# A layered kernel whose last attention stage adds its causal mask on DVE instead of by products on PE

## The chip, the cores and the metric

The kernel runs on one core of one Trainium2 chip. The metric is the device time of one execution in microseconds (us). PE is the matrix engine, DVE the vector engine, ACT the activation engine, POOL the GpSimd engine and SP the engine that issues most DMAs. PSUM, the memory that PE writes its products to, is used as eight banks, each of 512 float32 per partition.

## The reference, cut to what matters

Four layers follow each other on x of 4 batches x 1024 positions x 128 channels: x = x + attention(norm(x)) + feed-forward(norm(x)). The change is in the last layer, whose attention has 16 heads of 8 channels and a causal mask, beside a mixture of 8 experts with the two best per token:

```python
# layer 3: b = 4, s = 1024, h = 16, hd = 8
qkv = (x @ W_qkv + b_qkv).reshape(b, s, h, 3 * hd)
...
logits = jnp.einsum('bshd,bkhd->bhsk', q, k) / np.sqrt(hd)
mask = k_pos > q_pos
logits = jnp.where(mask[None, None, :, :], -jnp.inf, logits)
attn = jax.nn.softmax(logits, axis=-1)
out = jnp.einsum('bhsk,bkhd->bshd', attn, v).reshape(b, s, d)
return out @ W_out + b_out
```

## The kernel before, in words

`layer3` runs a norm, a front stage that makes q, k, v and the routing of the experts, and `attn3_stage`, where attention, experts and output projection run together. All of the change is in `attn3_stage`.

The attention is cut into 16 items: 4 batches, each with 4 groups of 4 heads. An item passes through three slots, so that slot s has three items in work. In slot s the *first pass* of item s makes the scores of each query against the keys that it may see, and takes the largest of each row. In slot s + 1 the maxima are turned (`turn_max`, `turned_max`), split into three bfloat16 parts on POOL (`split_max`) and sent by DMA into extra rows of the q tile. In slot s + 2 the *second pass* makes the same scores the other way round, keys on the partitions and the maximum already subtracted by those extra rows (`scoreT`, L2194); ACT takes the exponential (`exps`, L2329), POOL zeroes what is masked on the diagonal (`causal`, L2509), and PE sums with v (`sums`, L2209). So there are 18 slots: slots 0 and 1 have only a first pass (and in slot 1 the turn of the maxima), slots 2 to 15 have both passes, slots 16 and 17 only the second.

The first pass of an item is 20 units (S0 to S19 below). A unit is one tile of 128 queries (t = 0 to 7) against up to 512 keys, for two row groups r of the array (partitions 0 to 63 and 64 to 127, `HROW`), and for one or both of two head pairs e. PE (`score`, L2167) writes a unit into two neighbouring banks; DVE (`largest`, L2379) reduces it with one maximum. Units S0 and S1 (t = 0, 1), S8 (the last 128 keys of t = 4) and S11 (the last 256 of t = 5) hold both e; S2 to S5, S14, S15, S18 and S19 are diagonal units of one e. These 12 of 20 units end on the diagonal: their last 128 keys hold a square in which the keys above the diagonal are in the future. In it, before the change, PE adds the mask with four more products per e (L2172): identity times `maskneg_q` (-1e30 above the diagonal, else 0), in two halves of 64 rows, for each r. The constants for it are loaded by four DMAs and cast to bfloat16 by POOL.

The order on each engine is written out by hand. A slot has 12 groups g; `SHARE` says how many units of the first pass stand in each: 2, 2, 1, 1, 2, 2, 2, 2, 2, 2, 1, 1. Between them stand the second pass, and, in slots 2 to 13, the 39 expert tiles: `turn_rows` (XT, at the start of the slot, read by the DVE copy L2406), `up` (a burst after group 4, L2236, followed by `gelu` on ACT with an activation table of its own), and `down` (groups 7 to 10, L2246, read by the DVE copy L2412). `turn_sums` (X, L2218) turns an item's result for `norm` on DVE (L2394, L2399).

Two rings of banks tie the engines. The S ring has two places of two banks each, and everything that DVE reads goes through it in one order: Z (the turned maxima), the S units, XT, X, DOWN and the output projection. Before PE writes entry n of this ring it waits until DVE has read entry n - 2. The other ring has three banks, between PE's second pass and ACT. Every engine runs its instructions in order, so a PE instruction that waits for DVE also holds back the second-pass products behind it. The next slot begins with Z, which waits for the reduction over the maxima (`a_m`, L2470), and this for the last unit.

Of the kernel before, what the change touches and what calls it, by code (L numbers as in the profile page):

```python
# [18 lines left out]
BF16 = mybir.dt.bfloat16  # L19
# [3 lines left out]
P = 128  # L23
# [75 lines left out]
class Kit:  # L99
# [14 lines left out]
    def sb(self, name, shape, dt=F32, ctx=None):  # L114
        return (ctx or self.ctx).enter_context(self.nc.sbuf_tensor(name, shape, dt))
# [1798 lines left out]
HROW = (0, 64)  # L1914
# [86 lines left out]
def attn3_stage(k, R):  # L2001
# [15 lines left out]
    with ExitStack() as ctx:  # L2017
        sb = lambda x, shape, dt=F32: k.sb("a3_" + x, shape, dt, ctx=ctx)
        qs = [sb(f"q{u}", [P, 2, S], BF16) for u in range(4)]
        ks = [sb(f"k{u}", [P, 2, S], BF16) for u in range(4)]  # L2020
        consts, constsb = sb("consts", [P, 2, 2, P]), sb("consts_bf16", [P, 2, 2, P], BF16)
        mx = sb("mx", [P, 2, 2, 2, QT, 2])
        m = sb("m", [P, 2, 2 * 2 * QT])
        mT, mr = sb("mT", [32, 2, P]), sb("mr", [32, 2, P])
# [38 lines left out]
        with nc.Block() as block:  # L2063
            @block.sync
            def _(sp):
                for r in range(2):
                    for n, src in enumerate(("ident", "maskneg_q")):
                        sp.dma_start(consts[HROW[r]:HROW[r] + 64, n, :, :],
                                     ins[src].rearrange("(a p) q -> p a q", p=64)).then_inc(s_c, 16)
                for dst, src in ((wo[:], ins["L3a_wout"]), (b2[0:NE], ins["L3f_b2"]),  # L2070
                                 (b2[NE:NE + 1], ins["L3a_bout"].rearrange("(a n) -> a n", a=1))):
                    sp.dma_start(dst, src).then_inc(s_o, 16)
# [51 lines left out]
                for s in range(SLOTS):  # L2124
# [8 lines left out]
                        store_tile(kt)  # L2133
                    if 3 <= s + 2 < NI:
                        stacks(s + 2)
                sp.wait_ge(s_c, 64)
                sp.wait_ge(s_o, 48)
                for u in range(4):
                    sp.wait_ge(s_qk[u], 16 * 4 * len(RUNS) * NI // 4)
# [3 lines left out]

            @block.tensor
            def _(pe):
                pe.wait_ge(ready, 9)
                pe.wait_ge(o_zero, 1)

                def take_s(*key):
# [6 lines left out]
                def score(c, i):  # L2156

                    t, es, x, w = SU[i]
                    u = c % 4
                    if i == 0:  # L2160
                        pe.wait_ge(s_qk[u], 16 * 4 * len(RUNS) * (c // 4 + 1))
                    bank = take_s("S", c, i)
                    diag = x + w == (t + 1) * P
                    for j, e in enumerate(es):
                        for r in range(2):
                            rows = slice(HROW[r], HROW[r] + KROWS)
                            mm = pe.matmul(k.ps[:, bank + r, j * w:j * w + w], qs[u][rows, e, t * P:t * P + P],  # L2167
                                           ks[u][rows, e, x:x + w], start=True, stop=not diag, skip_group_check=True)
                        for half in range(2 if diag else 0):
                            for r in range(2):  # L2170
                                rows = slice(HROW[r], HROW[r] + 64)
                                mm = pe.matmul(k.ps[:, bank + r, j * w + w - P:j * w + w],  # L2172
                                               constsb[rows, 0, half, :], constsb[rows, 1, half, :],
                                               start=False, stop=half == 1, skip_group_check=True)
                    mm.then_inc(s_done, 1)

                def turn_max(c):
# [181 lines left out]
            def _(dve):  # L2359
                dve.memset(k.ps[:, bankO, :], 0.0).then_inc(o_zero, 1)  # L2360
                dve.memset(mx[:], -3e38).then_inc(mx_zero, 1)
                dve.wait_ge(mx_zero, 1)
                n_i = itertools.count(1)
                last = {}

                def arrived(*key):

# [4 lines left out]
                def largest(c, i):  # L2372

                    t, es, x, w = SU[i]
                    if i == 0 and c >= 2:
                        dve.wait_ge(max_done, c - 1)
                    bank = arrived("S", c, i)
                    src = k.ps[:, bank:bank + 2, 0:len(es) * w].rearrange("p r (e k) -> p r e k", k=w)
                    dve.tensor_reduce(mx[:, c % 2, :, es[0]:es[0] + len(es), t, x // CH], src, AX_X, ALU.max)\  # L2379
                       .then_inc(s_read, 1)  # L2380

# [94 lines left out]
            def _(pool):  # L2476
                for u in range(4):
                    for r in range(2):
                        pool.memset(ks[u][HROW[r] + 32:HROW[r] + 64, :, :], 1.0).then_inc(ready, 1)
                        pool.wait_ge(ready, 2 * u + r + 1)  # L2480
                pool.wait_ge(s_c, 64)
                pool.tensor_copy(constsb[:], consts[:]).then_inc(ready, 1)
                n_p = itertools.count(1)

                def split_max(c):

                    def step(one):
                        one.then_inc(split, 1)
                        pool.wait_ge(split, next(n_p))

                    u = c % 2
                    if c == 0:
                        pool.wait_ge(ready, 9)
                    if c >= 2:
                        pool.wait_ge(masked, (c - 1) * len(DIAG))
                    pool.wait_ge(s_read, s_at["Z", c] + 1)
                    if c > 0:
                        pool.wait_ge(s_m[(c - 1) % 4], 16 * 6 * ((c - 1) // 4 + 1))
                    step(pool.tensor_copy(mp[:, 0, :], mT[:, u, :]))
                    step(pool.tensor_tensor(mr[:, 0, :], mT[:, u, :], mp[:, 0, :], ALU.subtract))  # L2500
                    step(pool.tensor_copy(mp[:, 1, :], mr[:, 0, :]))
                    step(pool.tensor_tensor(mr[:, 1, :], mr[:, 0, :], mp[:, 1, :], ALU.subtract))
                    pool.tensor_copy(mp[:, 2, :], mr[:, 1, :]).then_inc(parts, 1)
# [185 lines left out]
```

## Time and profile before

| | us |
|---|---|
| median of 3 runs | 2866.93 |
| lowest and highest | 2866.49 to 2872.39 |
| the profiled execution's own time | 2862.31 |
| its span, first to last instruction | 2860.6 |
| attention stage: first unit to the end of slot 15's first pass | 2061.0 to 2750.1 |

Mean granted TensorE clock 0.846 of full speed. The span lies 1.7 us under the execution's own time, and that execution lies 4.6 us under the median. A row of the timeline gives start, duration, engine, line, operation, the tiles (out<-in) with shapes and how many instructions are merged; a bracket says how long the engine was idle just before and which instruction ended it. A row of a stretch gives the busy time of each engine in it, and the granted clock.

### The profile page before, as it was taken

To read this page: it belongs to the slowest core of one execution; us is meant where nothing else is said; L and a number is where in the kernel's file an instruction comes from. 1 tells how busy PE (TensorE), PEld (TensorE's weight loads), DVE (VectorE), ACT (ScalarE), POOL (GpSimd) and SP (SyncE) were. 2 spreads that over 40 slices of the span, in tenths; PEclk is the share of its full clock that TensorE was granted. 3 is DMA by queue.
4 is the path that set the end of the run, shared out by engine and by line. 5 is a ranking of instruction groups with operands and counts; after the bars stand their busy time and mean duration, and the time that the engine had idled before them with its cause. 6 is when DMAs were issued, how large, how long until landed. Compare 5 with 4: busy or idle time off the path is not lost. (4 is left out here: it accounts for less than half of the span.)

```text
span 2860.6 us, 35232 instructions
## 1 busy us (share of the span) xinstructions
PE 2053.1 (72%) x10366; PEld 1065.6 (37%) x10366; DVE 1900.9 (66%) x2468; ACT 1428.5 (50%) x2507; POOL 1366.1 (48%) x990
## 2 busy tenths in 40 slices
PE   2698787897977668566635888851178888888875
PEld 1233333333333244243414666641034444444312
DVE  6299999999999966833256777762175555555641
ACT  1476677777767527133414333323036556656453
POOL 2299989998999940220024666517201111111353
PEclk9899999998999979687766888965569999999866
DMA  1344444444545520012100000004222222222111
GB/s 31 88 152 143 154 148 139 155 153 137 157 140 156 152 63 0 1 52 72 37 0 0 0 0 0 0 11 99 82 61 80 75 72 81 66 79 57 35 26 49
DMA packets 146983, 214.72 MB, mean 75 GB/s; under 512 B 30746, under 2 KB 58292, under 8 KB 146228
## 3 DMA queue, kind: packets, MB, share of 16 engines
q1 hardware_dynamic: 142756, 204.72, 23.7%
q0 software_dynamic: 4096, 8.40, 1.4%
q8 instruction: 64, 1.05, 0.2%
q14 instruction: 67, 0.55, 0.1%
HBM read 193.91 MB, written 23.86 MB: 76 GB/s over the span
## 5 line engine op out<-in xcount | busy, mean ns | idle before, releaser
L513 PE MATMUL ps<-m_hC,ident 128*128 128x512 f32 x1024 | 510.2, 642 | 136.6 <-DVE m_hC L795 136.6
L711 POOL TENSOR_TENSOR m_dBx<-m_du,m_rowB 128x1024 f32<-128x1024 f32 x256 | 603.8, 2387 | 7.0 <-DMA m_rowB<-bc_rows 6.8
L2329 ACT ACTIVATE a_pT<-ps 128x512 f32<-128x512 f32 (+2 forms) x640 | 319.7, 553 | 398.1 <-PE ps L2194 396.7
L2379 DVE TENSOR_REDUCE a_mx<-ps 128x2 f32<-128x1024 f32 (+2 forms) x320 | 349.3, 1116 | 168.8 <-PE ps L2172 128.1
L637 ACT ACTIVATE ps<-m_delta,m_A 128x512 f32<-128x512 f32 x512 | 339.7, 685 | 120.2 <-DVE m_h L786 119.3
L513 PEld LDWEIGHTS ps<-m_hC,ident 128*128 128x128 f32 x1024 | 202.2, 205 | 429.4 <-issue 229.0
L2509 POOL TENSOR_SCALAR_AFFINE_SELECT a_pT<-a_pT 128x512 f32<-128x512 f32 x128 | 81.5, 636 | 522.8 <-ACT a_pT L2329 522.3
L786 DVE TENSOR_TENSOR_SCAN m_h<-ps,m_carry,m_dBx 128x512 f32<-128x512 f32 x256 | 311.2, 1266 | 9.0 <-ACT ps L637 9.0
L786 DVE TENSOR_TENSOR_SCAN m_h<-ps,m_dBx 128x512 f32<-128x512 f32 x256 | 295.9, 1206 | 18.8 <-ACT ps L637 18.2
L795 DVE TENSOR_TENSOR m_hC<-m_h,ps 128x1024 f32<-128x1024 f32 x176 | 214.9, 1221 | 23.0 <-ACT ps L647 7.2
L721 POOL TENSOR_TENSOR m_hC<-m_h,m_rowC 128x1024 f32<-128x1024 f32 x80 | 194.4, 2430 | 71.0 <-DVE m_h L786 70.7
L2167 PE MATMUL ps<-a_k,a_q 48*128 48x512 bf16 (+3 forms) x768 | 141.0, 369 | 110.7 <-DMA a_k<-qk_parts 94.3
L2209 PE MATMUL ps<-a_pT,l_v 128*9 128x512 f32 (+3 forms) x1536 | 189.6, 570 | 22.6 <-POOL a_pT L2509 22.6
L2194 PE MATMUL ps<-a_q,a_k 51*128 51x512 bf16 (+3 forms) x768 | 131.4, 367 | 68.7 <-ACT a_pT L2329 67.3
L647 ACT COPY ps<-m_rowC 128x512 f32<-128x512 f32 x176 | 102.9, 585 | 126.6 <-DVE m_hC L795 125.9
L1629 PE MATMUL ps<-c_triu_adt,ones 128*128 128x512 f32 x64 | 53.6, 934 | 92.0 <-ACT c_triu_adt L1600 92.0
L468 PE MATMUL ps<-pad,m_wk 128*128 128x512 f32 x256 | 117.3, 603 | 1.1 <-DVE m_diag L744 1.1
L2194 PEld LDWEIGHTS ps<-a_q,a_k 51*128 51x128 bf16 x768 | 32.6, 95 | 193.8 <-ACT a_pT L2329 158.3
L266 PE MATMUL ps<-ident,n_xn 128*128 128x128 f32 x128 | 35.3, 431 | 84.2 <-DVE n_xn L246 83.8
L1907 POOL DMA_INDIRECT expert_rows<-l_xn,l_slot x64 | 65.3, 1020 | 62.0 <-DVE p_cmp L1873 42.8
L1078 POOL TENSOR_TENSOR acc<-acc,b_o 128x512 f32 x8 | 11.2, 1402 | 170.8 <-ACT acc L1068 170.8
L2167 PEld LDWEIGHTS ps<-a_k,a_q 48*128 48x128 bf16 x768 | 40.2, 100 | 130.4 <-issue 94.8
(361 smaller groups left out, 3927.8 us busy)
## 6 DMA issues: line engine op xcount, KB each, us to landing
m_rowB<-bc_rows SPq DMA_DIRECT2D x256, 256.0 KB, 4.5
m_rowC<-bc_rows SPq DMA_DIRECT2D x256, 256.0 KB, 4.0
a_w<-in_L3f_w1T SPq DMA_DIRECT2D x39, 256.0 KB, 2.5
a_w<-in_L3f_w2T SPq DMA_DIRECT2D x39, 256.0 KB, 3.2
qk_parts<-p_part SPq DMA_DIRECT2D x24, 256.0 KB
expert_rows<-in_zero_rows SPq DMA_DIRECT2D x39, 128.0 KB, 2.7
a_xs<-expert_rows SPq DMA_DIRECT2D x39, 128.0 KB, 2.1
expert_out<-a_y SPq DMA_DIRECT2D x39, 128.0 KB, 3.2
```

The lines of the kernel that those rows point to most:

```text
L468: mm = pe.matmul(o, wk[:, d, tap, c * P:c * P + P], pad[:, b * ROW + shift:b * ROW + shift + CH], start=tap == 0, stop=tap == CONV - 1)
L513: mm = pe.matmul(ps[:, bankY + c, :], k.ident[:], hC[:, n % NBUF, c, :], start=False, stop=n % NS == NS - 1)
L637: act.activation(ps[:, bankA + m % 3, :], delta[:, i % 2, c, chunk(i, x)], ACT.Exp, scale=An[:, ITEMS[i][0], c, s:s + 1]).then_inc(decayed, 1)
L711: pool.tensor_tensor(dBx[:, n % NBUF], du[:, i % 2, :, chunk(i, x)], rowB[:, n % 4, :].unsqueeze(1).to_broadcast([P, HALF, CH]), ALU.mult) ...
L721: pool.tensor_tensor(hC[:, n % NBUF], h[:, n % NBUF], rowC[:, n % 4, :].unsqueeze(1).to_broadcast([P, HALF, CH]), ALU.mult).then_inc(hc_po ...
L786: dve.tensor_tensor_scan(time(h[:, n % NBUF, c, :]), time(ps[:, bankA + m % 3, :]), time(dBx[:, n % NBUF, c, :]), first, ALU.mult, ALU.add ...
L795: dve.tensor_tensor(hC[:, n % NBUF], h[:, n % NBUF], ps[:, bankC, :].unsqueeze(1).to_broadcast([P, HALF, CH]), ALU.mult).then_inc(hc_dve, 1)
L2167: mm = pe.matmul(k.ps[:, bank + r, j * w:j * w + w], qs[u][rows, e, t * P:t * P + P], ks[u][rows, e, x:x + w], start=True, stop=not diag, ...
L2194: mm = pe.matmul(k.ps[:, tbank(n + r), j * w:j * w + w], ks[u][rows, e, kt * P:kt * P + P], qs[u][rows, e, q0:q0 + w], start=True, stop=Tr ...
L2209: mm = pe.matmul(k.ps[32 * hd:32 * hd + HD + 1, bankO, CH - w:CH], R["v"][:, c, kt, hd, :], pT[:, g % 3, hd, 0:w], start=kt == 0, stop=kt ...
L2329: act.activation(dst, src, ACT.Exp).then_inc(t_read, 1)
L2379: dve.tensor_reduce(mx[:, c % 2, :, es[0]:es[0] + len(es), t, x // CH], src, AX_X, ALU.max)\
```

## The change

PE's mask products, their constants, the four DMAs and POOL's cast are gone. The mask is loaded once in float32. DVE, before the maximum of each of the 12 diagonal units, adds the mask to the square in the score banks (PSUM in, PSUM out) with one instruction for both r and the e of the unit, waits for its own result, and then reduces as before. 192 additions in 16 items take the place of 1024 products in the records.

```diff
-        consts, constsb = sb("consts", [P, 2, 2, P]), sb("consts_bf16", [P, 2, 2, P], BF16)
+        maskneg, hidden = sb("maskneg", [P, P]), k.sem("a3_hidden")
...
-                for r in range(2):
-                    for n, src in enumerate(("ident", "maskneg_q")):
-                        sp.dma_start(consts[HROW[r]:HROW[r] + 64, n, :, :],
-                                     ins[src].rearrange("(a p) q -> p a q", p=64)).then_inc(s_c, 16)
+                sp.dma_start(maskneg[:], ins["maskneg_q"]).then_inc(s_c, 16)
...
-                pe.wait_ge(ready, 9)
+                pe.wait_ge(ready, 8)
...
-                                           ks[u][rows, e, x:x + w], start=True, stop=not diag, skip_group_check=True)
-                        for half in range(2 if diag else 0):
-                            for r in range(2):
-                                rows = slice(HROW[r], HROW[r] + 64)
-                                mm = pe.matmul(k.ps[:, bank + r, j * w + w - P:j * w + w],
-                                               constsb[rows, 0, half, :], constsb[rows, 1, half, :],
-                                               start=False, stop=half == 1, skip_group_check=True)
+                                           ks[u][rows, e, x:x + w], start=True, stop=True, skip_group_check=True)
...
+                dve.wait_ge(s_c, 16)
...
+                    if x + w == (t + 1) * P:
+                        square = src[:, :, :, w - P:w]
+                        future = maskneg[:].unsqueeze(1).unsqueeze(1).to_broadcast([P, 2, len(es), P])
+                        dve.tensor_tensor(square, square, future, ALU.add).then_inc(hidden, 1)
+                        dve.wait_ge(hidden, next(n_h))
...
-                pool.wait_ge(s_c, 64)
-                pool.tensor_copy(constsb[:], consts[:]).then_inc(ready, 1)
...
-                    if c == 0:
-                        pool.wait_ge(ready, 9)
```

On DVE, at the start of slot 3 (a slot with both passes and expert tiles), the order before is, with `a_mT` the turned maxima, `a_mx` the row maxima and `a_xT` the turned expert rows:

```order
L2386 TENSOR_SCALAR a_mT<-ps 32x128
L2379 TENSOR_REDUCE a_mx<-ps 128x4 x2
L2406 COPY a_xT<-ps 128x256
L2379 TENSOR_REDUCE a_mx<-ps 128x2 x2
L2406 COPY a_xT<-ps 128x256
L2379 TENSOR_REDUCE a_mx<-ps 128x2
L2406 COPY a_xT<-ps 128x256
```

and with the change (the same lines stand four to ten lines earlier in the file):

```order
L2382 TENSOR_SCALAR a_mT<-ps 32x128
L2373 TENSOR_TENSOR ps<-ps,a_maskneg 128x2x256
L2375 TENSOR_REDUCE a_mx<-ps 128x4
L2373 TENSOR_TENSOR ps<-ps,a_maskneg 128x4x128
L2375 TENSOR_REDUCE a_mx<-ps 128x4
L2402 COPY a_xT<-ps 128x256
L2373 TENSOR_TENSOR ps<-ps,a_maskneg 128x2x128
L2375 TENSOR_REDUCE a_mx<-ps 128x2
L2373 TENSOR_TENSOR ps<-ps,a_maskneg 128x2x128
L2375 TENSOR_REDUCE a_mx<-ps 128x2
L2402 COPY a_xT<-ps 128x256
```

Each of the diagonal units has an addition in front of its reduction; nothing else changes place. On PE, at the start of slot 2, the order before is, with L2180 the turn of the maxima and L2194 the second pass:

```order
L2180 MATMUL ps<-ident,a_m 32x128
L2194 MATMUL ps<-a_q,a_k 128x512 x2
L2167 MATMUL ps<-a_k,a_q 128x128 x2
L2172 MATMUL ps<-a_consts_bf 128x128 x4
L2167 MATMUL ps<-a_k,a_q 128x128 x2
L2172 MATMUL ps<-a_consts_bf 128x128 x4
L2194 MATMUL ps<-a_q,a_k 128x512 x2
```

and with the change:

```order
L2170 MATMUL ps<-ident,a_m 32x128
L2184 MATMUL ps<-a_q,a_k 128x512 x2
L2163 MATMUL ps<-a_k,a_q 128x128 x4
L2184 MATMUL ps<-a_q,a_k 128x512 x2
L2163 MATMUL ps<-a_k,a_q 128x256 x4
```

The mask products are gone, and the products around them follow each other directly.

## Rows read from the trace of the kernel before

**Rows 1.** The page, part 1: busy time, share of the span, instructions of each engine.

```profile
PE 2053.1 (72%) x10366; PEld 1065.6 (37%) x10366; DVE 1900.9 (66%) x2468; ACT 1428.5 (50%) x2507; POOL 1366.1 (48%) x990
```

**Rows 2.** Busy time of each engine by stretch, slots 0, 7, 14, 15. Columns: stretch, length, busy (instructions), clock, DMA.

```profile
2061.00:2083.40 22.40, 14.54 (x112) 5.66 (x112) 21.20 (x21) 0.00 (x0) 0.00 (x0) 0.50 0.18 56
2343.00:2385.60 42.60, 35.83 (x343) 18.47 (x343) 25.78 (x33) 27.99 (x56) 6.75 (x13) 1.00 0.22 62
2667.70:2712.10 44.40, 37.63 (x313) 15.52 (x313) 27.16 (x33) 20.92 (x42) 19.77 (x27) 0.85 0.14 39
2712.10:2750.10 38.00, 29.81 (x257) 8.81 (x257) 23.71 (x28) 20.84 (x42) 19.72 (x27) 0.78 0.10 26
```

**Rows 3.** All products of line L2172: duration ns min/median/max, first and last start.

```profile
L2172 PE MATMUL ps<-a_consts_bf x1024: 213/216/312, 2061.1 to 2748.4; 64*128 64x128 bf16 x171
```

**Rows 4.** DVE in slots 0 and 1, in order of time.

```profile
2062.74 20.49 DVE L2379 TENSOR_REDUCE a_mx<-ps 128x4 f32<-128x1024 f32 x19
...
2085.65 20.49 DVE L2379 TENSOR_REDUCE a_mx<-ps 128x4 f32<-128x1024 f32 x19 [0.16 <-PE ps L2172]
```

**Rows 5.** DVE timeline: what additions, waits and a write to PSUM take.

```profile
2035.15 0.48 DVE L2360 MEMSET ps<- 128x512 f32 x1 [35.49 <-PEq L1746]
...
2330.26 0.69 DVE L2426 TENSOR_TENSOR x_tm<-x_tm,ps 128x512 f32<-128x512 f32 x1 [2.90 <-PE ps L2270]
2330.87 2.35 DVE L2379 TENSOR_REDUCE a_mx<-ps 128x2 f32<-128x1024 f32 x2
...
2368.58 0.26 DVE L2394 RECIPROCAL a_rs<-ps 128x16 f32<-128x16 f32 x1 [0.33 <-PE ps L2218]
2368.88 0.29 DVE L2399 TENSOR_TENSOR a_att<-ps,a_rs 128x128 f32<-128x128 f32 x1
```

**Rows 6.** Start of slot 7, PE and DVE, in order of time.

```profile
2343.17 0.27 PE L2180 MATMUL ps<-ident,a_m 128*32 128x128 f32 x1 [0.82 <-DVE a_m L2470]
...
2343.48 0.28 DVE L2386 TENSOR_SCALAR a_mT<-ps 32x128 f32<-32x128 f32 x1 [0.45 <-PE ps L2180]
...
2344.22 0.69 DVE L2379 TENSOR_REDUCE a_mx<-ps 128x4 f32<-128x512 f32 x1 [0.46 <-PE ps L2172]
...
2345.33 1.23 DVE L2379 TENSOR_REDUCE a_mx<-ps 128x4 f32<-128x1024 f32 x1 [0.42 <-PE ps L2172]
...
2347.11 1.82 DVE L2379 TENSOR_REDUCE a_mx<-ps 128x2 f32<-128x768 f32 x2 [0.22 <-PE ps L2172]
...
2349.55 1.23 DVE L2379 TENSOR_REDUCE a_mx<-ps 128x2 f32<-128x1024 f32 x1 [0.24 <-PE ps L2172]
...
2350.83 0.66 PE L2218 MATMUL ps<-ident,a_oT 128*128 128x128 f32 x4 [0.20 <-DVE a_mx L2379]
...
2354.47 2.86 PE L2236 MATMUL ps<-a_xT,a_w 128*128 128x256 f32 x12
```

**Rows 7.** End of slot 7, PE and DVE.

```profile
2382.27 0.38 PE L2167 MATMUL ps<-a_k,a_q 48*128 48x512 bf16 x2
2382.49 0.28 PE L2172 MATMUL ps<-a_consts_bf 64*128 64x128 bf16 x4
...
2382.81 2.54 DVE L2379 TENSOR_REDUCE a_mx<-ps 128x2 f32<-128x1024 f32 x2 [0.24 <-PE ps L2172]
...
2385.75 0.27 PE L2180 MATMUL ps<-ident,a_m 128*32 128x128 f32 x1 [0.82 <-DVE a_m L2470]
```

**Rows 8.** Starts of slots 2, 7 (to the burst) and 14, stretches as in rows 2.

```profile
2106.50:2120.50 14.00, 13.18 (x111) 4.94 (x111) 8.78 (x12) 7.15 (x15) 4.21 (x9) 0.63 0.09 27
2343.10:2354.40 11.30, 9.87 (x123) 4.25 (x123) 9.13 (x14) 7.49 (x16) 4.21 (x9) 1.00 0.23 66
2668.00:2681.00 13.00, 8.92 (x117) 3.60 (x116) 9.21 (x11) 8.20 (x17) 10.27 (x16) 0.96 0.32 91
```

**Rows 9.** PE in slot 14, the same products at either level of the clock.

```profile
2681.14 1.11 PE L2255 MATMUL ps<-ident,a_att 128*128 128x128 f32 x4
...
2686.97 0.66 PE L2255 MATMUL ps<-ident,a_att 128*128 128x128 f32 x4
```

More of the change, by code:

```diff
@@ L2135, in _ @@
                         stacks(s + 2)
-                sp.wait_ge(s_c, 64)
+                sp.wait_ge(s_c, 16)
                 sp.wait_ge(s_o, 48)
@@ L2162, in score @@
                     bank = take_s("S", c, i)
-                    diag = x + w == (t + 1) * P
                     for j, e in enumerate(es):
@@ L2362, in _ @@
                 dve.wait_ge(mx_zero, 1)
-                n_i = itertools.count(1)
+                n_i, n_h = itertools.count(1), itertools.count(1)
                 last = {}
+                dve.wait_ge(s_c, 16)
                 def arrived(*key):
```

## The prediction

> **What bounds the kernel now.** I read the page's busy times first [rows 1]: over the whole span PE and DVE lead with 72% and 66%, so no average decides. The change touches only the last attention stage, so I cut that into its slots [rows 2]. Three kinds stand out. In slots 0 and 1 (first pass alone) DVE is busy 21.2 of 22.4 us, and its timeline shows 19 reductions without a gap in 20.49 us in each of the two [rows 4]: DVE is the bound, and PE waits for it. In slots 2 to 13, of which slot 7 is the type, PE is busy 35.8 of 42.6 us, DVE 25.8, ACT 28.0: PE's order is the spine, and it stops where ACT or DVE is late. Slots 14 and 15 have no expert tiles, but POOL, with 19.7 us, stands in PE's way. Then I read the start and the end of slot 7 in order of time [rows 6, 7]. At the start DVE has hardly any slack: between the turned maxima, read at 2343.76 (2343.48 + 0.28), and the reduction of unit S4 at 2350.78 (2349.55 + 1.23), it idles 0.46 + 0.42 + 0.22 + 0.24 = 1.34 us of 7.0, and PE's X (L2218) already waits 0.20 for it. Between the groups 5 and 10 it has much slack. At the end Z waits 0.82 us for the maxima.
>
> **What an addition costs.** No row shows an addition from PSUM into PSUM. The nearest one adds 512 elements from PSUM into SBUF in 0.69 us, a product of 128 elements takes 0.29 [rows 5]. The line through the first two gives 0.29 + 0.40 x 128/384 = 0.42 for 256. A diagonal unit of one e has 256 elements in its squares (2 r x 128), one of two e 512. The wait for its own result has a row too: the product of L2399 waits for the reciprocal in front, and starts 0.30 after the latter's start of 0.26, that is 0.04 after its end; two reductions without a wait start 2.35 - 1.23 = 1.12 apart, so 0.1 before the end of the first. The addition itself may start overlapped in that way; the reduction behind it may not. In a chain without gaps an addition therefore puts its duration and 0.04 on top: 0.46 for 256 elements and 0.73 for 512. An item has 8 of the first and 4 of the second: 3.7 + 2.9 = 6.6 us.
>
> The page "VectorE: DVE Perf Modes" of the Trainium skill (The DRAIN you can't avoid) says that the next operation waits for the pipe to empty anyway and that a semaphore in between costs nothing extra. The rows speak against it: 0.1 us of overlap without a wait, a gap of 0.04 with one. By the page an addition would put some 0.13 less on the chain, 1.6 us less an item, and the sum below would be about 10 us smaller; I go by the rows.
>
> The bounds of an addition: not under a write of 512 elements into PSUM alone, 0.48, and for 256 not under the 0.29 of the 128-element one [rows 5]; with the gap, 0.52 and 0.33, which is 4.7 us an item. Not over one that passes its elements twice, for reading and writing the same banks: 0.69 for 256 and 1.23 for 512 (the 1024-element reduction), with the gap 0.73 and 1.27, 10.9 us an item. I take 6.6, the same operation with another destination.
>
> **What PE gives back.** 1024 products of 216 ns [rows 3] overlap each other. What they add is how much later the last of them ends: in unit S18, 2382.49 + 0.28 = 2382.77 against 2382.27 + 0.38 = 2382.65 without [rows 7], 0.12 us per e. An item has 16 such e, 1.8 us at full clock.
>
> **Slots 0 and 1.** DVE's chain grows by 6.6 us in each, and all of it is on the path, since PE waits for the banks. At the start of either the mask products leave the front of the first reduction; with the clock at half (0.50, rows 2) they take about twice 0.12 per e, so 0.4 for the first unit and a little for the second. I count 6.2 + 6.0 = +12.2 us.
>
> **Slots 2 to 13, the start.** S0 to S4 bring two additions of 0.73 and three of 0.46: 2.8 us before S4 is read. Of the 1.34 us of idle time in this chain all close but 0.2 (DVE starts S0 that much after the turned maxima are read): 1.1 us. So S4 is read 1.7 us later. PE's X is entry n + 2 of the ring and now waits for it; what stands behind X on PE, in order, is the second pass of groups 3 and 4, units S5 to S7 and the burst of expert products that starts at 2354.47 [rows 6]. ACT takes its scores from that second pass and gets them 1.7 late as well. The mask products taken off PE here buy nothing, as PE waits at each entry. +1.7.
>
> **The middle.** In groups 5 to 9 DVE waits for PE by microseconds, so the additions of S8, S11, S14 and S15 lie beside PE's work, but for 0.2 us at S12, which stands two entries behind S11. PE saves the masks of these units; at S8 and S14 a wait for ACT follows at once and takes the saving, at S11 and S15 (0.24 + 0.12) it stays: PE comes to S18 0.3 earlier (S12's 0.2 is caught within PE's wait for ACT behind it).
>
> **The end.** S18 and S19 bring 0.92 us of additions. 0.12 goes since S18 reaches DVE earlier, 0.2 since its two reductions have a gap between them (2.54 against 2.35 for two in a row, rows 7 and 5). So the maxima, and Z behind them, come 0.6 later; with the 0.3 saved upstream +0.3. A slot costs 1.7 + 0.3 = 2.0 us, twelve 24 us.
>
> **Slots 14 to 17.** POOL's mask and DMA issues hold PE up more than DVE does, and there is no XT. The additions hide, and PE at a lower clock (0.85 and 0.78, rows 2) keeps something of its 1.8 us: -1.5 in all. The rest is untouched. The removed cast and DMAs lie before the q and k stacks land, which is what PE's first product waits for: nothing. The mask's DMA lands long before the first unit.
>
> The sum of work is 12.2 + 24 - 1.5 = +34.7 us.
>
> **The clock.** It moves between 1.2 and 2.4 GHz. Slot 2 runs to its burst at a granted 0.63, mostly the lower level, and takes 14.0 us for what slot 7 does in 11.3 at 1.00 [rows 8]: 2.7 us. In slot 14 PE is busy 8.9 of the first 13 us, and right behind them the same four transposes take 1.11 instead of 0.66 us, the lower level [rows 8, 9]; 6 us later they are fast again. In slot 7 it is busy 9.9 us up to the burst; with the change the masks of S0 to S5 leave this stretch (8 e, 1.0 us) and it becomes 1.7 longer: 8.9 of 13 us, as in slot 14. So the clock may fall in slots 2 to 13 too, where it now stays up. What falls into the DVE-bound start costs nothing, what reaches the burst up to 2.7 us; ACT, with 4 to 5 us of gelu in it, covers part. I take 0.5 us a slot, +6, between 0 and 12 x 2.7 = 32.
>
> The forecast is +41 us: 2862.3 + 41 = 2903 for an execution like the profiled one, and, as that lies 4.6 under the median, 2908 for the median.
>
> **Rivals.**
> *The clock falls in every slot.* For it speaks slot 14, against it that slots 2 to 13 hold more PE work than slot 14 and that the fall may land where DVE is the bound. 34.7 + 32 = +67: 2934. The page "TensorE: Matmul & The Clock Gate" of the Trainium skill (Part 1) says that the throttled state is the default and that activity releases it; slot 14 agrees. It is this rival's rule.
> *PSUM to PSUM costs double.* 10.9 an item: slots 0 and 1 +8.6 more; S0 to S4 2 x 1.27 + 3 x 0.73 = 4.7 instead of 2.8, the end 0.5 more, 12 x 2.4 = 29. 41 + 38 = +79: 2946. For it speaks only that no row shows the form.
> *Faster: PE is the bound and DVE's slack swallows the additions.* DVE is idle 16.8 us in slot 7, more than 6.6. If the delay at a slot's start were caught up before Z, PE would keep 1.8 us in each of 14 slots, -25, against 12.2 in slots 0 and 1: -13, 2854. It decides the other way once S4's read is more than 0.2 us or so late, since X already waits for it; and for catching up the middle would need PE idle that is not ACT's.
> *No change.* Slots 2 to 15 give back just the 12.2 of slots 0 and 1: 0.9 us each, half of the masks; 2867.
>
> Chances: forecast 0.58, clock 0.20, double price 0.10, faster 0.05, no change 0.04, and 0.03 for more than +79. About 0.2% (5.7 us) is what a measurement of this kernel tells from no change. Slower 0.91, within 0.04, faster 0.05. Downwards the lower price takes 3.8 us off slots 0 and 1, and 0.8 at a start and 0.3 at an end, x 12 = 13, off the others, and a clock that stays up takes off 6: 2885 for both together. The forecast's own range is 2890 to 2930. To hold 8 in 10 it takes in the clock rival: 2890 to 2938.
>
> **What would show it.** Right: L2373 takes 0.42 and 0.69 us; slots 0 and 1 are 6 us longer each; in slots 2 to 13 X (now L2208) waits 1 to 2 us for DVE, the burst starts 13 us after Z, and the slots are 2 to 3 us longer; slots 14 and 15 keep their length. Wrong: an addition of 1.2 us for 512 elements; granted clock under 0.9 in slots that had 1.00, with slots 4 us longer; or Z in slots 3 to 13 at its old distance, with DVE idle before it.

## The result, and the profile after

The changed kernel takes 2914.28 us (median of 4 runs, 2906.21 to 2920.22), the one before beside it 2868.38 (2866.49 to 2872.39). The ratio is 1.0156, 95% interval 1.0129 to 1.0184: slower by 46 us. The forecast was 2908 and 2890 to 2930. The profiled execution took 2915.11 with a span of 2913.4 us, so against the profiled one before the span is 52.8 us longer, where 41 were forecast. (Between executions of one kernel the clock of PE falls at different places.)

The page's busy times, to set beside [rows 1]:

```profile
PE 2062.0 (71%) x9342; PEld 1027.7 (35%) x9342; DVE 1994.7 (68%) x2660; ACT 1429.9 (49%) x2507; POOL 1365.8 (47%) x989
```

DVE gained 94 us of work and PE lost 1024 instructions, yet PE's busy time rose by 9: a product that runs at the lower clock counts for longer (0.61 us instead of 0.39 below). What an addition takes stands in the view of line L2373 (duration in ns, min/median/max), the operation that no row showed before:

```profile
L2373 DVE TENSOR_TENSOR ps<-ps,a_maskneg x192: 420/432/700, 2060.4 to 2800.1; 128x256 f32<-128x256 f32 x128, 128x512 f32<-128x512 f32 x64
```

0.42 to 0.43 us for 256 elements and 0.70 for 512, PSUM to PSUM, as the line through [rows 5] gave it. The slots, with the columns of [rows 2], again slots 0, 7, 14 and 15:

```profile
2061.00:2087.98 26.98, 10.31 (x40) 1.93 (x40) 26.45 (x33) 0.00 (x0) 0.00 (x0) 0.50 0.11 37
2369.78:2415.20 45.42, 36.83 (x279) 16.59 (x279) 31.63 (x44) 28.12 (x56) 6.75 (x13) 0.92 0.21 63
2717.38:2763.73 46.35, 38.76 (x249) 14.10 (x249) 32.92 (x44) 21.08 (x42) 19.91 (x27) 0.77 0.13 35
2763.73:2802.13 38.40, 29.11 (x201) 6.25 (x201) 29.58 (x39) 20.95 (x42) 19.99 (x28) 0.72 0.10 27
```

In slots 0 and 1 DVE has hardly a gap, and now an addition stands before each diagonal reduction:

```profile
2063.60 0.42 DVE L2373 TENSOR_TENSOR ps<-ps,a_maskneg 128x256 f32<-128x256 f32 x1
2064.05 0.96 DVE L2375 TENSOR_REDUCE a_mx<-ps 128x2 f32<-128x768 f32 x1
2064.93 0.42 DVE L2373 TENSOR_TENSOR ps<-ps,a_maskneg 128x256 f32<-128x256 f32 x1
...
2087.68 0.22 DVE L2466 TENSOR_REDUCE a_m<-a_mx 128x32 f32<-128x64 f32 x1
...
2116.07 0.22 DVE L2466 TENSOR_REDUCE a_m<-a_mx 128x32 f32<-128x64 f32 x1
```

From one addition to the reduction behind it pass 0.45 us, and the next addition starts 0.08 before that reduction ends: what [rows 4, 5] led to expect. The maxima of item 1 come 28.4 us after those of item 0, before 22.9.

The span's 52.8 us split as follows. Places are read from the two timelines: the first DVE instruction of the stage, the Z of each slot (L2180 before, L2170 after), the end.

| part | before | after | difference | forecast |
|---|---|---|---|---|
| all before the first unit is read | 2061.95 | 2060.39 | -1.6 | -0.4 |
| slot 0, first read unit to Z | 21.7 | 27.7 | +6.0 | +6.6 |
| slot 1 | 22.9 | 28.4 | +5.5 | +6.0 |
| slots 2 to 13 | 561.3 | 601.0 | +39.7 | +24 and 6 for the clock |
| slots 14 and 15 | 82.9 | 85.2 | +2.3 | -1.5 |
| behind them | 109.9 | 110.8 | +0.9 | 0 |

The first row is not the change: over the traces of all kernels in this document the first unit is read at 2052 to 2064 us, and in a second trace of the changed kernel (e9) at 2063.3.

The start of slot 7, PE first; the rows answer to [rows 6]:

```profile
2369.84 0.27 PE L2170 MATMUL ps<-ident,a_m 128*32 128x128 f32 x1 [1.50 <-DVE a_m L2466]
2370.04 0.39 PE L2184 MATMUL ps<-a_q,a_k 51*128 51x512 bf16 x2
...
2371.12 0.61 PE L2184 MATMUL ps<-a_q,a_k 51*128 51x512 bf16 x2 [0.57 <-ACT a_pT L2319]
...
2374.21 0.50 PE L2163 MATMUL ps<-a_k,a_q 48*128 48x384 bf16 x2 [0.46 <-DVE a_mx L2375]
...
2377.93 0.38 PE L2163 MATMUL ps<-a_k,a_q 48*128 48x512 bf16 x2
...
2380.11 0.65 PE L2208 MATMUL ps<-ident,a_oT 128*128 128x128 f32 x4 [0.66 <-DVE a_mx L2375]
...
2383.69 1.56 PE L2226 MATMUL ps<-a_xT,a_w 128*128 128x256 f32 x6
```

and DVE's additions in it:

```profile
2370.66 0.70 DVE L2373 TENSOR_TENSOR ps<-ps,a_maskneg 128x512 f32<-128x512 f32 x1 [0.23 <-PE ps L2163]
2371.39 0.69 DVE L2375 TENSOR_REDUCE a_mx<-ps 128x4 f32<-128x512 f32 x1
2372.20 0.70 DVE L2373 TENSOR_TENSOR ps<-ps,a_maskneg 128x512 f32<-128x512 f32 x1
...
2374.76 0.43 DVE L2373 TENSOR_TENSOR ps<-ps,a_maskneg 128x256 f32<-128x256 f32 x1 [0.27 <-PE ps L2163]
...
2378.36 0.43 DVE L2373 TENSOR_TENSOR ps<-ps,a_maskneg 128x256 f32<-128x256 f32 x1
2378.82 1.23 DVE L2375 TENSOR_REDUCE a_mx<-ps 128x2 f32<-128x1024 f32 x1
```

X (L2208) comes 10.3 us after Z instead of 7.7 and waits 0.66 for DVE; the burst (L2226) comes 13.9 after Z instead of 11.3. Z itself had waited 1.50 us for the maxima instead of 0.82. But a second thing is to be seen. The same pair of products of the second pass takes 0.39 us at 2370.04 and 0.61 at 2371.12, behind a wait of 0.57 for ACT: the clock has gone to its lower level, 1.3 us into the slot. At 2377.9 the products are fast again (0.38 for 512 columns). The stretch of 9.5 us from Z on shows it in its granted clock, here for slots 7 and 9, with all of slot 9 behind them:

```profile
2369.84:2379.34 9.50, 8.47 (x57) 2.40 (x57) 7.98 (x13) 5.51 (x11) 3.00 (x8) 0.64 0.24 72
2462.94:2472.44 9.50, 8.57 (x51) 2.32 (x55) 7.25 (x12) 5.07 (x11) 2.94 (x7) 0.50 0.40 112
2462.94:2516.78 53.84, 46.30 (x305) 21.16 (x306) 32.91 (x46) 29.80 (x60) 6.75 (x13) 0.81 0.23 66
```

and, for comparison, the start of slot 7 and the whole of slot 9 in the kernel before:

```profile
2343.17:2352.67 9.50, 8.61 (x109) 3.98 (x111) 7.40 (x12) 6.03 (x13) 3.78 (x9) 1.00 0.28 79
2429.60:2476.21 46.61, 39.96 (x370) 22.10 (x370) 26.61 (x34) 29.64 (x60) 6.75 (x13) 1.00 0.28 77
```

Before, 9 of the 11 starts of slots 3 to 13 had a granted clock of 1.00; after, none had (0.50 to 0.67). The end of slot 7, to set beside [rows 7]:

```profile
2411.58 0.43 DVE L2373 TENSOR_TENSOR ps<-ps,a_maskneg 128x256 f32<-128x256 f32 x1
...
2412.05 1.23 DVE L2375 TENSOR_REDUCE a_mx<-ps 128x2 f32<-128x1024 f32 x1
...
2413.19 0.42 DVE L2373 TENSOR_TENSOR ps<-ps,a_maskneg 128x256 f32<-128x256 f32 x1
...
2413.64 1.23 DVE L2375 TENSOR_REDUCE a_mx<-ps 128x2 f32<-128x1024 f32 x1
...
2415.27 0.37 PE L2170 MATMUL ps<-ident,a_m 128*32 128x128 f32 x1 [1.45 <-DVE a_m L2466]
```

The two reductions now have an addition before each, and Z comes where the addition of S19 puts it.

### The profile page after: what moved, and what is told of

Read it like the earlier page. It is cut to its first block and busy times, and to the rows that moved or that the text cites. A ratio compares the mean times of both kernels' runs of the same rounds, so it can differ in the third digit from the quotient of the medians.

```text
span 2913.4 us, 33371 instructions
## 1 busy us (share of the span) xinstructions
PE 2062.0 (71%) x9342; PEld 1027.7 (35%) x9342; DVE 1994.7 (68%) x2660; ACT 1429.9 (49%) x2507; POOL 1365.8 (47%) x989
## 3 DMA queue, kind: packets, MB, share of 16 engines
q1 hardware_dynamic: 142324, 204.53, 23.3%
## 5 line engine op out<-in xcount | busy, mean ns | idle before, releaser
L2375 DVE TENSOR_REDUCE a_mx<-ps 128x2 f32<-128x1024 f32 (+2 forms) x320 | 351.7, 1117 | 39.6 <-PE ps L2163 31.6
L2199 PE MATMUL ps<-a_pT,l_v 128*9 128x512 f32 (+3 forms) x1536 | 208.7, 623 | 17.9 <-POOL a_pT L2501 16.4
L2184 PE MATMUL ps<-a_q,a_k 51*128 51x512 bf16 (+3 forms) x768 | 141.1, 394 | 77.3 <-ACT a_pT L2319 71.6
L2373 DVE TENSOR_TENSOR ps<-ps,a_maskneg 128x256 f32<-128x256 f32 (+1 forms) x192 | 99.1, 516 | 106.6 <-PE ps L2163 102.7
```

What stands on the lines that cost most here:

```text
L2184: mm = pe.matmul(k.ps[:, tbank(n + r), j * w:j * w + w], ks[u][rows, e, kt * P:kt * P + P], qs[u][rows, e, q0:q0 + w], start=True, stop=Tr ...
L2199: mm = pe.matmul(k.ps[32 * hd:32 * hd + HD + 1, bankO, CH - w:CH], R["v"][:, c, kt, hd, :], pT[:, g % 3, hd, 0:w], start=kt == 0, stop=kt ...
```

## The experiments

All variants of the mask keep both ways in one source and choose by unit: where PE masks, the products are those of before; where DVE masks, the addition of the change. "X" and "burst" below are times after Z in the profiled execution; "starts at 1.00" counts, in the 11 slots from 3 to 13, those whose first 9.5 us have a granted clock of 1.00. The sums were made by adding the slots of each trace. A ratio is taken beside runs of the kernel before on the same chip: e1 to e4 on one chip, e5 to e8 on a second, e9 to e12 on a third. The ratio is of all runs, the other columns are of one execution, which need not be a typical one: that of e2 took 2855.3 us where the median of its kernel is 2870.3, and that of e10 2894.0 where the median is 2903.8.

| kernel | ratio to before, 95% | starts at 1.00 | Z to burst, slots 2 to 13 | burst to next Z | slot 1 |
|---|---|---|---|---|---|
| before | 1 | 9 of 11 | 144.5 | 416.8 | 22.9 |
| changed | 1.0156, 1.0129 to 1.0184 | 0 | 170.4 | 430.6 | 28.4 |
| changed, again (e9) | 1.0150, 1.0120 to 1.0180 | 0 | 169.9 | 426.2 | 28.4 |
| both (e1) | 1.0166, 1.0136 to 1.0196 | 3 | 173.5 | 425.1 | 28.9 |
| neither (e2) | 1.0011, 0.9993 to 1.0028 | 2 | 152.2 | 412.6 | 22.0 |
| PE for items 0, 1 (e3) | 1.0148, 1.0113 to 1.0182 | 0 | 171.0 | 430.2 | 22.9 |
| DVE in the middle (e4) | 0.9999, 0.9981 to 1.0018 | 8 | 144.1 | 409.2 | 22.9 |
| changed, filled at Z (e5) | 1.0111, 1.0070 to 1.0153 | 0 | 169.0 | 416.5 | 28.7 |
| DVE at the start (e6) | 1.0059, 1.0033 to 1.0086 | 0 | 168.5 | 409.5 | 25.4 |
| DVE at the end (e7) | 1.0041, 1.0011 to 1.0071 | 2 | 158.4 | 423.6 | 23.8 |
| before, filled (e8) | 0.9962, 0.9937 to 0.9987 | 11 | 138.7 | 413.3 | 23.3 |
| changed, filled throughout (e10) | 1.0127, 1.0100 to 1.0153 | 8 | 169.3 | 414.9 | 28.7 |
| middle, filled (e11) | 0.9967, 0.9949 to 0.9984 | 11 | 139.4 | 410.7 | 23.3 |
| neither, filled (e12) | 0.9978, 0.9955 to 1.0001 | 4 | 148.7 | 412.9 | 22.4 |

### Both sides' work, and neither's

The theory after the result was that PE's waits for DVE bring the clock down (A); its rival, that the products PE lost do (B). Two kernels cross the factors: in one both functions below return True, in the other both False.

```diff
-                    diag = x + w == (t + 1) * P
+                    diag = x + w == (t + 1) * P and pe_masks(c, i)
...
+                    if x + w == (t + 1) * P and dve_masks(c, i):
+                        square = src[:, :, :, w - P:w]
...
+                        dve.tensor_tensor(square, square, future, ALU.add).then_inc(hidden, 1)
```

> PE keeps its mask products and DVE adds the mask as well (the mask is added twice, which leaves the same keys hidden). In the changed kernel the granted clock falls to its lower level at the start of nearly every slot from 2 to 13, and X there comes 10.2 to 11.0 us after Z instead of 7.7. Theory A: the fall comes from PE's waits for DVE (the longer wait of Z, the waits in the ring). Then it stays when PE has its products back: X at 10 to 11 us in most slots, time 2910 to 2930, ratio to before 1.015 to 1.022. Rival B: the fall comes from the products that PE lost. Then the clock stays up at the starts, X comes at 9.4 us (7.7 + 1.7 by DVE's work alone), and the time is 2895 to 2905, ratio 1.009 to 1.013.

> No mask at all in the first pass: no products on PE and no additions on DVE; the maxima are then taken over the future keys of the diagonal squares too, the second pass is untouched. Theory A: with nothing added to DVE, PE's waits are as before, the clock stays up at the starts, X comes at 7.4 to 7.7 us, a slot from 2 to 13 is 0.3 us shorter, and slots 0 and 1 are unchanged within 1 us: ratio 0.996 to 0.999. Rival B: PE's missing products let the clock fall at the starts as in the changed kernel, each costing about 2.6 us: ratio 1.005 to 1.010.

Both: 1.0166, inside A's range. But 3 of 11 starts kept their clock, and they show what both engines' work costs without a fall. Slot 4's first 9.5 us, and PE's waits in it:

```profile
2215.17:2224.67 9.50, 7.08 (x85) 3.00 (x85) 8.07 (x13) 5.47 (x11) 3.58 (x8) 1.00 0.35 102
```

```profile
2219.56 0.34 PE L2177 MATMUL ps<-a_k,a_q 48*128 48x384 bf16 x2 [1.16 <-DVE a_mx L2395]
...
2225.16 0.66 PE L2228 MATMUL ps<-ident,a_oT 128*128 128x128 f32 x4 [0.66 <-DVE a_mx L2395]
```

At a clock of 1.00 S2 waits 1.16 us for DVE, and X comes at 10.0 us (slots 4, 8, 12: 9.99, 10.01, 10.00), 2.3 later than before; B's 9.4 was too low. PE here still makes its mask products, and DVE waits for them; without them X comes at 9.56 at this clock (e10 below).

Neither: 1.0011, between A's and B's ranges. In two starts (slots 4 and 11) the clock stayed up and X came at 7.4 us, as A has it; in the other nine it fell with no addition anywhere. Slots 7 and 4:

```profile
2333.47:2342.97 9.50, 8.66 (x57) 2.40 (x57) 5.89 (x8) 5.50 (x11) 3.00 (x8) 0.64 0.34 79
2188.03:2197.53 9.50, 8.22 (x79) 2.82 (x79) 7.68 (x12) 6.11 (x14) 4.01 (x9) 1.00 0.43 128
```

and Z and X of slot 7:

```profile
2333.47 0.27 PE L2190 MATMUL ps<-ident,a_m 128*32 128x128 f32 x1 [0.59 <-DVE a_m L2486]
...
2343.26 0.66 PE L2228 MATMUL ps<-ident,a_oT 128*128 128x128 f32 x4 [0.20 <-DVE a_mx L2395]
```

PE works 8.66 of 9.5 us there and X is at 9.8 us. So neither factor is needed for a fall and each brings some: without the products 9 of 11 starts fell, with the additions 8, where the kernel before has 2. Both theories were half right. A kernel without any mask in its first pass is not faster than the one before. That is not for want of a saving: slot 11, which runs at 1.00 throughout, takes 41.7 us, where the kernel before takes 42.6 in slot 7, of the same kind and at the same clock. But from Z to burst the twelve slots take 7.7 us more than before, by the falls.

### Items 0 and 1 masked by PE

```diff
+def pe_masks(c, i):  return c < 2
+def dve_masks(c, i): return c >= 2
```

> PE masks items 0 and 1 as before, DVE the other 14. If slots 0 and 1 cost what the chain of DVE says, this is 12 us less than the changed kernel: ratio to before about 1.011, slots 0 and 1 at 22.4 and 22.9 us again. If PE's idle time there were the bound, nothing would change (1.0156).

Slot 1 in this kernel:

```profile
2085.69:2108.60 22.91, 14.77 (x114) 5.66 (x114) 21.55 (x22) 0.00 (x0) 1.68 (x5) 0.50 0.46 135
```

22.91 us, and slot 0 takes 21.7 again: in the profiled execution the two give 11 us back, so their price is shown. The ratio of 1.0148 lies 2 us, not 12, under the 1.0156 of the change. In this trace slots 14 and 15 took 4 us more than in that of the changed kernel, and the first unit was read 3.7 later, at 2064.0; the intervals overlap widely, and the total time doesn't decide.

### DVE masks the middle units

```diff
+def pe_masks(c, i):  return c < 2 or i not in (8, 11, 14, 15)
+def dve_masks(c, i): return c >= 2 and i in (8, 11, 14, 15)
```

> From item 2 on DVE masks units S8, S11, S14 and S15 alone, which stand where DVE waits for PE; PE masks all others. Theory: DVE hides the additions, PE keeps 0.36 us in each of slots 2 to 13 and about 1 us in slots 14 and 15 together: ratio 0.997 to 1.000. Rival: the stalls that DVE's additions bring lower the clock there as well: ratio over 1.003.

0.9999. In the trace slots 2 to 13 are 8 us shorter (553.2 against 561.3), slots 14 and 15 3 longer. At a clock of 1.00 the part of a slot behind the burst takes 30.94 us instead of 31.28, 0.34 less where 0.36 was worked out; twelve times that is 4 of the 8 us, and the rest is falls at other places. The additions hide, as expected; whether a gain is left in the whole time is below what this measurement tells.

### The start alone, the end alone

```diff
# e6: S0 to S5 by DVE
+def dve_masks(c, i): return i <= 5
# e7: S18 and S19 by DVE
+def dve_masks(c, i): return i in (18, 19)
```

> DVE masks S0 to S5 only, PE all others. Theory: the start carries most of the loss. Slots 0 and 1 +3.8 us each (2 x 0.73 + 4 x 0.47 = 3.3 and a little), slots 2 to 13 +2.5 us each by X at 10 us or more, together +35 to +40: ratio 1.012 to 1.014. If the clock at a start hangs mainly on the longer wait of Z at the end of the slot before, X comes at 9.4 to 10 us at a clock of 1.00: ratio 1.007 to 1.010.

> DVE masks S18 and S19 only, PE all others. Slots 0 and 1 +0.9 us each. By DVE's work alone Z comes 0.65 us later: +8 in twelve slots, +10 in all, ratio 1.003 to 1.004. If the longer wait of Z is what brings the clock down, X comes at 10 us in most slots instead of 7.7 and the ratio is 1.010 to 1.014.

The start alone gives 1.0059, under both theories' ranges. Slot 1 is 2.5 us longer than before, not 3.8. X is at 9.9 to 10.5 us and the clock at 0.64 to 0.82 in all starts, as the first had it, but behind the burst the slots are faster: 31.3 us in five of the six slots of slot 7's kind (3, 4, 7, 8, 11, 12), where the kernel before has that in two and 32.5 to 34.0 in the others. What the theory missed is that here falls at the start went with fewer falls after the burst. That is no rule: in the changed kernel all starts fell too, and four of those six slots fell behind the burst as well (32.8 to 34.3 us instead of 31.6). Slots 14 and 15 were 7 us shorter, which the additions don't explain.

The end alone gives 1.0041, near the first range (1.003 to 1.004). The profiled execution, at 2881.9, is 9 us over the median of this kernel. The slots behind the burst take 31.92 us where they took 31.28, +0.64 as worked out for S18 and S19. But the start now falls in 9 of 11 slots, in 7 of them to an X of 9.9 to 10.3 us, which is what the rival had named for the longer wait of Z, without the rival's ratio. Slot 7's Z and X, and its first 9.5 us:

```profile
2352.24 0.27 PE L2190 MATMUL ps<-ident,a_m 128*32 128x128 f32 x1 [1.45 <-DVE a_m L2486]
...
2362.50 0.66 PE L2228 MATMUL ps<-ident,a_oT 128*128 128x128 f32 x4 [0.19 <-DVE a_mx L2395]
```

```profile
2352.24:2361.74 9.50, 9.11 (x83) 3.58 (x83) 5.42 (x8) 5.35 (x11) 2.94 (x7) 0.64 0.29 72
```

Z waits 1.45 us instead of 0.82, and X comes at 10.3 us with no more of a wait for DVE (0.19) than in the kernel before (0.20), whose X is at 7.7 us: here it is the clock alone.

### Products without use in PE's waits

```diff
+                def fill(c, bank, n):
+                    for _ in range(n):
+                        pe.matmul(k.ps[:, bank, :], qs[c % 4][0:KROWS, 0, 0:P], ks[c % 4][0:KROWS, 0, 0:CH],
+                                  start=True, stop=True, skip_group_check=True)
                 def turn_max(c):
                     bank = take_s("Z", c)
+                    fill(c, bank + 1, 5)
...
+                            if front and back and g == 5 and i == 2 and tiles_of(s):
+                                fill(f, take_s("S", f, 9), 5)
```

e5 has the first of the two fillings, e8 both, with 4 instead of 5 at Z.

> The changed kernel, and PE runs five products without use (q by k, 512 columns, into the free bank of Z's pair, overwritten later) ahead of Z, in the time in which it waits for the maxima. They take 1.1 us at full clock, and Z waits 1.9 us there. If the falls of the clock at the starts come from how little PE works around Z, whoever took the work away, the granted clock in the first 9.5 us of slots 2 to 13 is 1.00 in most, X comes at 9.7 to 10.0 us, and the time is 15 to 30 us under the changed kernel: ratio to before 1.005 to 1.010. If the falls come from the waits inside the start (for ACT and for DVE's reads), the filler changes nothing: 1.014 to 1.018.

> The kernel before with four such products ahead of Z and five ahead of the second pass of group 5, where PE waits 2 us for ACT's table load. If what PE does in its waits sets the clock, it is 1.00 almost throughout slots 3 to 13 (before: 0.91 to 1.00) and these slots get 42.3 us long where three tiles and no projection stand in them: 10 to 18 us less in all, ratio 0.994 to 0.997. If not, 1.000 or, as the products delay PE at the lower clock, up to 1.003.

In the changed kernel Z's wait is filled, and the start falls all the same (slot 9, Z, X and the first 9.5 us):

```profile
2449.08 0.28 PE L2176 MATMUL ps<-ident,a_m 128*32 128x128 f32 x1 [0.18 <-DVE a_m L2472]
...
2459.38 0.66 PE L2214 MATMUL ps<-ident,a_oT 128*128 128x128 f32 x4 [0.66 <-DVE a_mx L2381]
```

```profile
2449.08:2458.58 9.50, 8.47 (x57) 2.39 (x57) 7.95 (x13) 5.51 (x11) 2.96 (x8) 0.64 0.43 107
```

The starts did what the second theory had, and the falls at the changed kernel's starts don't hang on Z's wait. Yet the ratio is 1.0111, between both ranges. In this trace slots 8 to 10, which had a clock of 0.81 to 0.86, have 0.89 to 0.91, the time from burst to Z went from 430.6 to 416.5 us, and slots 14 and 15 took 76.7 instead of 85.2. Whether that is a gain over the changed kernel isn't settled: its interval (1.0129 to 1.0184, on another chip) overlaps this one's.

In the kernel before, the same filling keeps all 11 starts at 1.00, and the ratio is 0.9962, faster by 11 us (0.9937 to 0.9987), as expected; the slots of slot 7's kind take 42.7 us, not 42.3. Slot 7, its start and the whole:

```profile
2340.67:2350.17 9.50, 8.61 (x109) 3.98 (x111) 7.38 (x12) 6.03 (x13) 3.76 (x9) 1.00 0.37 79
2340.67:2383.35 42.68, 37.83 (x353) 19.14 (x353) 25.76 (x32) 28.00 (x56) 6.75 (x13) 1.00 0.26 66
```

### The changed kernel with all waits filled

```diff
+                                if back and tiles_of(s) and (g, i) in ((1, 0), (2, 0)):
+                                    fill(f, turned[0] + 1, 3 if g == 1 else 2)
                                 score(f, units[i // 2])
...
+                                fill(f, turned[0] + 1, 2)
                             turn_sums(b - 1, 1)
```

These stand ahead of S2, S4 and X and write the other half of XT's pair; e5's and e8's fillings, five each, are in it too. (`fill` here reads the rows of row group 1 when it writes an odd bank.)

> The changed kernel once more, beside the others of this group on one chip: ratio to before 1.013 to 1.018, its starts at a clock of 0.50 to 0.67 and X at 10.2 to 11.0 us.

> The changed kernel with products without use in every wait of the start (three ahead of S2, two ahead of S4, two ahead of X, in the unused half of XT's bank pair), five ahead of Z and five ahead of the second pass of group 5. Theory: DVE's chain bounds the start at X = 10.0 us whatever the clock, so a clock kept at 1.00 there gives back only 0.3 to 0.5 us a start, and the rest comes from the falls behind it: slots 2 to 13 at 580 to 586 us, ratio 1.008 to 1.011. Rival: the clock is the larger part of the start's loss, X comes at 8.5 to 9.5 us and the ratio is under 1.006. If the products only delay PE at the lower clock: 1.013 or more.

On the same chip the changed kernel itself gave 1.0150, as expected, with X at 10.1 to 11.0 us. With its waits filled it keeps the clock at 8 of 11 starts and measures 1.0127 (1.0100 to 1.0153), which that interval doesn't tell from 1.0150. The start of slot 4, the whole slot, its X, and the reduction of S4 in front of it:

```profile
2205.75:2215.25 9.50, 7.92 (x64) 2.51 (x64) 8.51 (x14) 5.38 (x11) 3.59 (x8) 1.00 0.36 109
2205.75:2250.39 44.64, 38.44 (x296) 17.45 (x296) 31.47 (x44) 28.00 (x56) 6.77 (x13) 1.00 0.24 70
```

```profile
2215.31 0.66 PE L2215 MATMUL ps<-ident,a_oT 128*128 128x128 f32 x4
```

```profile
2214.03 1.23 DVE L2390 TENSOR_REDUCE a_mx<-ps 128x2 f32<-128x1024 f32 x1
```

This is the changed kernel at an even clock: X at 9.56 us, burst at 13.15, a slot of 44.6 us (slots 3, 4 and 12: 44.7, 44.6, 44.6), where the kernel before at a clock of 1.00 takes 42.6. S4 has been read at 2215.26, 9.5 us after Z instead of 7.6, and X starts 0.05 later. So DVE's additions cost 1.9 us by X and 2.0 us by the slot, and no clock gives that back. (The addition of S4 waited 0.16 us for PE, which ran products without use before S4, so the 1.9 may hold up to that much of theirs.) Three starts (slots 6, 7, 11) still fell, and their X came at 11.1 to 12.6 us, with products without use in the fall. Even so slots 2 to 13 took 584.2 us, inside the theory's 580 to 586, and the profiled execution is 1.010 times the median before. The ratio of 1.0127, above the theory's 1.011, comes from the executions without a trace, whose median is 10 us longer; what they lost isn't known.

### The best version

> From item 2 on DVE masks S8, S11, S14 and S15 and PE the others, with the products without use ahead of Z (four) and of the second pass of group 5 (five). The kernel before with such products measured 0.9962. Here PE is spared 0.36 us a slot besides, 4 us in all: 0.994 to 0.996.

> No mask in the first pass at all (as in the run with neither side's work), and the same products without use in PE's waits. Without them the clock fell at 9 of 11 starts and the ratio was 1.0011. Theory: with the waits filled the clock stays up at most starts, X comes at 7.4 us, and the kernel shows what the masks cost at an equal clock: 0.990 to 0.994. If the falls at the starts need products inside the start, X stays at 9 to 9.8 us and the ratio at 0.998 to 1.001.

The middle units on DVE with filled waits: 0.9967, above the 0.994 to 0.996 expected and no better than the kernel before filled (0.9962 on another chip); slots 2 to 13 are 2 us shorter (550.1 against 552.0), slots 14 and 15 7.6 longer. Without any mask and filled: 0.9978, far from the theory's 0.990 to 0.994 and next to the other range (0.998 to 1.001). Only 4 of 11 starts kept their clock, and X is at 8.7 to 9.8 us in the others: lighter starts fell although Z's wait was filled. The lowest ratio is that of the kernel before with its waits filled; the three filled kernels' intervals overlap, so which is the fastest isn't told.

## Why the prediction was right

**The additions.** 0.42 and 0.69 us were forecast, 0.43 and 0.70 measured. The double price is out. Behind an addition, where DVE waits for it, the gap is 0.03 us; in front of it, without a wait, there are 0.08 of overlap. That is the rows' price of a wait, about 0.1 us. The page "VectorE: DVE Perf Modes" of the Trainium skill (The DRAIN you can't avoid) says that the semaphore costs nothing extra, and this chain speaks against it.

**Slots 0 and 1.** +12.2 was forecast, their own chains grew by 6.0 and 5.5, 11.5 in all, and PE masks in them bring slot 1 back to 22.9. Each lies about half a microsecond under its forecast. Part of that is idle time which the additions filled: in slot 1 of the kernel before DVE idled 0.48 and 0.16 us before its first two reductions, now 0.05 before the first addition.

**The start and the end of slots 2 to 13.** +1.7 and +0.3, 2.0 a slot, 24 in all. At an even clock the runs give +1.9 for X and +2.0 for the slot (e10), and the end alone +0.64 against 0.6 (e7). The step that S4's read sets X, and X all behind it, is shown (e10). The sign given for it, X waiting 1 to 2 us for DVE, did not come: in the changed kernel X waits 0.66 us in five of eleven slots and 0.35 or less in the others. PE meets the delay at several entries (in e1 at a clock of 1.00 S2 waits 1.16 and X 0.66), and part of it is hidden where PE itself runs at the lower clock. The middle hides its additions, as forecast: with DVE in S8, S11, S14 and S15 the time from burst to Z is 409 us, not more than before. That the saving there stays (0.34 us a slot at a clock of 1.00) is seen in the traces, not in the times.

**The clock.** This is the term that was mis-sized. Slots 2 to 13 cost 39.7 us, where 24 and 6 were forecast. In slots 2, 6 and 11 the kernel before had fallen at the start already (burst at 14.0, 13.8, 13.9 us), and there the additions added nothing (13.6, 14.1, 14.0): such a start takes about whichever is longer, PE's work at the lower clock or DVE's chain. (Slots 8, 9 and 12, at a clock of 0.50 to 0.51, took longer than either, 14.5 to 15.1.) In the other nine the burst came 2.5 to 3.4 us later, 25.9 in all, of which 9 x 1.85 = 17 are DVE's (e10) and 9 the clock's. Behind the bursts DVE's share is 0.3 a slot (31.58 against 31.28), 4 in all, and 10 of the 13.8 are the clock's. So, with DVE's share counted first, DVE brought 20 and the clock 19. Counted the other way round the clock's share is larger: in slots 6 and 11 before and in seven slots of e7, starts fell without an addition in them, and the burst came 2.2 to 2.6 us later. Nine such falls are about 22 of the 25.9 us, and leave 4 for the additions. The two causes overlap, and only the sum is a measurement. I had expected the fall at the burst, from the likeness to slot 14, and half an us a slot; it came inside the first 9.5 us and in every slot. That is the rival's event without its price: it asked for 2.7 on top of 2.0 in each slot, 4.7, and the slots cost 3.3 in the mean, since the fall lay where DVE's chain was the longer anyway. The prediction had also named a sign of being wrong: a clock under 0.9 in slots that had 1.00, with slots 4 us longer. That came true in two of the three slots that had 1.00 throughout, slot 5 (0.87, 5.3 us longer) and slot 9 (0.81, 7.2), and not in slot 7 (0.92, 2.9).

**Slots 14 and 15.** -1.5 was forecast, +2.3 came, at a clock of 0.77 and 0.72 instead of 0.85 and 0.78. That PE's saving was there and the lower clock took more is likely and not shown. Three variants (e5 to e7) had these slots shorter than before (75.6 to 80.4 us against 82.9), most others longer, up to 91.5; those three ran on one chip, where e8 took 83.9, and what sets these slots stays open.

**The rivals on the other side** fall with e1 and e10: the delay of a start is never caught up before Z. What DVE's 16.8 us of idle time in a slot hid was the middle alone.

**Luck.** Between the profiled executions the forecast was 12 us short, nearly all of it the clock and slots 14 and 15. That the medians differ by 46 us, close to the 41 forecast, owes part to which executions were drawn: those of the changed kernel lie 14 us apart. The work of DVE was forecast well; the clock was not, and the wide range held it.

What stays open is what brings a fall, and which execution falls where. The split between DVE and clock is from one profiled execution of each kernel, and executions of the same kernel differ by 14 us (changed, 4 runs), 24 us (before, 19 runs beside e1) and 35 us (before, 29 runs beside e5); the changed kernel's slots 2 to 13 took 601 us in one and 596 in another.

## What to carry to other kernels

Moving work to the engine with the lower busy share pays where that engine waits for the donor: here nearly all of DVE's 16.8 us of idle time in a slot lay behind the start, while the start of each slot ran on DVE's chain. So look at the idle time in front of the very instructions that are to grow. Work taken off PE bought nothing here: without any mask the clock fell at 9 of 11 starts instead of 2 and took back what was saved. Compare stretches of equal granted clock before calling anything a gain or loss. Where PE waits for a known time, a few products without use into a free bank were worth more (11 us) than leaving out the whole mask (no gain measured).

## What the hardware did that I had not expected

A fall of the clock needs no long wait. In slot 7 of the changed kernel PE had waited 1.50 us for Z and 0.57 for ACT, with 0.7 us of products between, when the products went from 0.39 to 0.61 us. Without any mask 9 of 11 starts fell, 7 of them with a Z wait of only 0.59 us, in slot 7 with PE busy 8.66 of 9.5 us by the record (much of it at the lower clock). "TensorE: Matmul & The Clock Gate" of the Trainium skill (Part 1) says that activity releases the throttle; the runs agree as far as 11 of 11 starts were kept by products without use (e8). But such products did not always hold the clock of the start behind them: in e5 they held none, in e12 4 of 11.

A kernel with less to do (1024 products fewer, and only one DMA more) was not faster: neither products nor additions measured 1.0011 (0.9993 to 1.0028).
